# Phases of three pairs, single banks and a two-bank operation for every third maximum, in an attention loop on one core

## The reference

```python
q = proj(Wq, bq)
k = proj(Wk, bk)
v = proj(Wv, bv)
attn = jnp.einsum('bhnd,bhmd->bhnm', q, k) * scale
attn = jax.nn.softmax(attn, axis=-1)
out = jnp.einsum('bhnm,bhmd->bhnd', attn, v)
```

## Time and profile before

| | us |
|---|---|
| median of three runs | 254.62 |
| profiled execution, its own time | 254.18 |
| its span, first to last instruction | 252.4 |
| PE busy | 238.2 (94%) |
| DVE busy | 194.9 (77%) |
| ACT busy | 178.6 (71%) |
| maxima on DVE, L1141, 128 of 1.22 | 155.3 |
| exp on ACT, L979, 232 of 0.60 | 126.0 |
| maxima's matmuls, L437, 256 | 92.7 |
| scores' matmuls, L472, 256 | 89.6 |
| values' matmuls, L530, 1024 records | 80.4 |

### The profile page before, as it was taken

The page is one execution under the profiler, slowest core; times in us unless marked ns, Lnnn a source line. Parts: engine busy times, 40 slices in busy tenths (PEclk is TensorE's granted clock), DMA queues, the critical chain, the costliest instruction groups (busy, mean ns, idle before and its releaser), DMA issues.

```text
span 252.4 us, 5599 instructions
## 1 busy us (share of the span) xinstructions
PE 238.2 (94%) x2105; PEld 109.6 (43%) x2106; DVE 194.9 (77%) x288; ACT 178.6 (71%) x366; POOL 46.4 (18%) x84
## 2 busy tenths in 40 slices
PE   8999998999999999999999999999989988789994
PEld 7455343333334333334343343333333875458420
DVE  2799788989889898898988989889502683359763
ACT  2736697888888888888888888888898132229610
POOL 7964099010010100101001210010100000000340
PEclk9999999999999999999999999999999999999999
DMA  4025300342112031440200000000000000000002
GB/s 135 0 79 170 94 0 4 84 171 68 40 47 68 23 85 39 100 168 5 95 1 3 1 3 2 4 0 4 1 4 1 3 0 3 0 3 0 1 0 86
DMA packets 6099, 10.06 MB, mean 40 GB/s; under 512 B 2240, under 2 KB 3840, under 8 KB 5944
## 3 DMA queue, kind: packets, MB, share of 16 engines
q1 hardware_dynamic: 6072, 9.70, 13.1%
HBM read 6.84 MB, written 2.62 MB: 37 GB/s over the span
## 4 chain that ended last, share of the span: by engine, by line
PE 79%; DVE 7%; POOL 5%; issue 4%; ACT 3%; DVEq 0%; POOLq 0%; ACTq 0%
PE psum L530 25%; PE psum L437 17%; PE psum L472 15%; PE psum L782 2%; PE psum L503 2%; DVE negmax L1141 2%; POOL qop L832 1%; POOL kop L832 1%; PE psum L382 1%; PE psum L540 1%; PE psum L402 1%; PE psum L691 1%; PE psum L496 1%; POOL early L912 1%; PE psum L414 1%
## 5 line engine op out<-in xcount | busy, mean ns | idle before, releaser
L1141 DVE TENSOR_REDUCE negmax<-psum 128x1 f32<-128x1024 f32 x128 | 155.3, 1224 | 14.9 <-PE psum L437 10.5
L979 ACT ACTIVATE probs<-psum 128x512 f32<-128x512 f32 x232 | 126.0, 598 | 19.9 <-PE psum L472 15.8
L437 PE MATMUL psum<-kop,qop 64*128 64x512 f32 x256 | 92.7, 444 | 0.6 <-DVE negmax L1141 0.3
L472 PE MATMUL psum<-qop,kop 64*128 64x512 f32 x256 | 89.6, 445 | 0.1
L530 PE MATMUL psum<-probs,v_aug 128*32 128x256 f32 x1024 | 80.4, 390 | 1.1
L472 PEld LDWEIGHTS psum<-qop,kop 64*128 64x128 f32 x256 | 37.1, 184 | 26.8 <-ACT probs L979 17.8
L437 PEld LDWEIGHTS psum<-kop,qop 64*128 64x128 f32 x256 | 37.6, 184 | 24.5 <-DVE negmax L1141 13.0
L530 PEld LDWEIGHTS psum<-probs,v_aug 128*32 128x32 f32 x1024 | 21.2, 108 | 42.2 <-ACT probs L979 27.2
L867 POOL TENSOR_TENSOR attn<-o_tok,rden 128x64 f32<-128x64 f32 x15 | 4.4, 297 | 105.5 <-DVE rden L1132 105.5
L931 POOL TENSOR_TENSOR early<-probs,early 128x512 f32<-128x512 f32 x4 | 5.1, 1274 | 50.2 <-ACT probs L1077 50.1
L540 PE MATMUL psum<-cbf_sb 128*128 128x256 bf16 x118 | 14.0, 273 | 0.0
(11 more groups left out here) (185 smaller groups left out, 183.4 us busy)
## 6 DMA issues: line engine op xcount, KB each, us to landing
parts_scratch<-early SPq DMA_DIRECT2D x4, 512.0 KB, 3.4
qop<-parts_scratch SPq DMA_DIRECT2D x28, 64.0 KB
vt_sb<-in_vt SPq DMA_DIRECT2D x1, 1024.0 KB, 4.9
kop<-parts_scratch SPq DMA_DIRECT2D x14, 64.0 KB
kop<-parts_scratch SPq DMA_DIRECT2D x28, 32.0 KB
x_sb<-in_x SPq DMA_DIRECT2D x2, 256.0 KB, 2.8
q_pair<-in_q_pairs SPq DMA_DIRECT2D x1, 512.0 KB, 3.3
qop<-max_row SPq DMA_DIRECT2D x28, 4.0 KB
```

The costliest lines, as they stand in the source:

```text
L437: last = nc.tensor.matmul(psum[:, 2 * (v % 2) + c, :], qop[at, b * PP + pp, qh * NH + t * P:qh * NH + (t + 1) * P], kop[at, b * PP + pp, c ...
L472: last = nc.tensor.matmul(psum[:, bank, :], kop[at, b * PP + pp, mt * P:(mt + 1) * P], qop[at, b * PP + pp, qh * NH:(qh + 1) * NH], start= ...
L979: last = nc.scalar.activation(probs[:, n % P_RING, h, :], psum[:, bank, :], ACT.Exp, scale=SCALE)
L1141: V.tensor_reduce(negmax[:, i, h * HT + t:h * HT + t + 1], psum[:, bank:bank + 2, :].rearrange("p a n -> p (a n)"), AX_X, ALU.max, negate= ...
```

## The change

Six things change together.

1. PE's order is written in pairs `p`, four per run, and in phases of three pairs (`PHASE`). Behind each phase come the values that are due: up to half unit p - 4 (`VALUES_LAG`), but never past the end of a block before the phase's end that reaches it (`values_goal`). That is one and a half units as a rule. At the end of a block the numbers are uneven, as the listing below shows.
2. `values(u, first, end)` can do half a unit: four matmuls over 128 columns instead of 256.
3. The four maxima banks are single: half m of a maximum goes to bank m modulo 4, and waits until half m - 4 is reduced.
4. DVE reduces the two halves of a maximum by two operations of 512 columns each (L1220 of the changed kernel), except for every third maximum, where one operation reads both banks and gives two columns (L1214). All go to `half_max`; when a block's maxima are there, one small operation takes the minimum of the two negated halves into `negmax` (L1224) and raises `maxima_done`, for which POOL waits instead of `slot_free`.
5. `CATCH_UP` is (0, 1), so the maxima run two units further ahead, and seven runs at the end have no maxima instead of six.
6. The transposes of maxima and of the output stand at the end of a phase, in front of its values. Before, those of the output also stood in front of values, behind two pairs, and those of the maxima behind values.

The core of the diff:

```diff
-CATCH_UP = (0,)
+PAIRS_OF = 2 * TOGETHER
+PHASE = 3
+VALUES_LAG = 4
+MAX_BANKS = 4
+ROWS_AHEAD = 3
+CATCH_UP = (0, 1)
...
+        for p in range(PAIRS_OF * RUNS):
+            wide = p >= WIDE_PAIR
+            if p % PAIRS_OF == PAIRS_OF - 1 if wide else ends_phase(p):
+                block_end = 2 * TT * (goal // (2 * TT) + 1)
+                goal = max(0, min(block_end, 2 * TOGETHER * (p // PAIRS_OF) if wide else p - VALUES_LAG))
+                values_goal[p] = goal
+                if goal == block_end:
+                    block_done[goal // (2 * TT) - 1] = p
+
+        def rows_pair(blk):
+
+            p = PAIRS_OF * (RUNS_OF * blk - ROWS_AHEAD) + PAIRS_OF - 1
+            return p if p >= WIDE_PAIR else phase_end_from(p)
...
+        def output_pair(blk):
+
+            p = block_done[blk]
+            return p + 2 * (PAIRS_OF if p >= WIDE_PAIR else PHASE)
...
+                m = HALVES * v + c
+                if m >= MAX_BANKS:
+                    pe.wait_ge(S["slot_free"], m - MAX_BANKS + 1)
                 if c == 0:
-                    if v >= 2:
-                        pe.wait_ge(S["slot_free"], v - 1)
...
-                last = nc.tensor.matmul(psum[:, 2 * (v % 2) + c, :],
+                last = nc.tensor.matmul(psum[:, m % MAX_BANKS, :],
...
-                if c == HALVES - 1:
-                    last.then_inc(S["slot_full"], 1)
+                last.then_inc(S["slot_full"], 1)
...
+            def values_until(n):
+
+                while half_units[0] < n:
+                    u, first = divmod(half_units[0], 2)
+                    end = 2 if first or half_units[0] + 2 <= n else 1
+                    values(u, first, end)
+                    half_units[0] += end - first
...
+            def after_pair(p):
+
+                small_work(p)
+                if p in values_goal:
+                    values_until(values_goal[p])
...
-                pool.wait_ge(S["slot_free"], TT * (blk + 1))
+                pool.wait_ge(S["maxima_done"], blk + 1)
...
-                dve.wait_ge(S["slot_full"], v + 1)
-                V.tensor_reduce(negmax[:, i, h * HT + t:h * HT + t + 1],
-                                psum[:, bank:bank + 2, :].rearrange("p a n -> p (a n)"), AX_X, ALU.max,
-                                negate=True).then_inc(S["slot_free"], 1)
+                at = h * HT + t
+                if v % PHASE == 0:
+                    dve.wait_ge(S["slot_full"], HALVES * (v + 1))
+                    first = HALVES * v % MAX_BANKS
+                    V.tensor_reduce(half_max[:, i, :, at], psum[:, first:first + HALVES, :], AX_X, ALU.max,
+                                    negate=True).then_inc(S["slot_free"], HALVES)
+                else:
+                    for c in range(HALVES):
+                        m = HALVES * v + c
+                        dve.wait_ge(S["slot_full"], m + 1)
+                        V.tensor_reduce(half_max[:, i, c, at:at + 1], psum[:, m % MAX_BANKS, :], AX_X, ALU.max,
+                                        negate=True).then_inc(S["slot_free"], 1)
+                if v % TT == TT - 1:
+                    dve.wait_ge(S["slot_free"], HALVES * (v + 1))
+                    V.tensor_tensor(negmax[:, i, :], half_max[:, i, 0, :], half_max[:, i, 1, :], ALU.min).then_inc(S["maxima_done"], 1)
```

More of the change, by code:

```diff
@@ L230, in scores_of, with ends_phase, phase_end_from @@
             return [(a, 0), (b, 0), (a, 1), (b, 1)] if max_jobs(g) else [(a, 0), (a, 1), (b, 0), (b, 1)]
[L232 to L240, removed]
+        def ends_phase(p):
+            return p % PHASE == PHASE - 1
+        def phase_end_from(p):
+            return p + (PHASE - 1 - p) % PHASE
@@ new lines, in conv_attn_hybrid_kernel @@
+        FIRST_WIDE = min(g for g in range(RUNS) if not max_jobs(g))
+        WIDE_PAIR = PAIRS_OF * FIRST_WIDE
+        values_goal, block_done = {}, {}
+        goal = 0
+        for p in range(PAIRS_OF * RUNS):
[6 more added lines that the diff above has]
+                    block_done[goal // (2 * TT) - 1] = p
@@ L242, in conv_attn_hybrid_kernel @@
         ST_JOBS = [("max_r", 0, 0)]
         for g in range(RUNS):
[L244 to L253, removed]
+            for i in range(PAIRS_OF):
+                p = PAIRS_OF * g + i
+                if g < FIRST_WIDE:
+                    ST_JOBS.append(("scores", *scores_of(g)[i]))
+                    ST_JOBS += small_jobs(p)
+                elif i % 2:
+                    ST_JOBS.append(("unit", p // 2, 0))
+                    if i == 1 and rows_within(g) is not None:
+                        ST_JOBS.append(("max_t", rows_within(g), 0))
@@ L254, in conv_attn_hybrid_kernel @@
+            if g >= FIRST_WIDE:
+                for p in range(PAIRS_OF * g, PAIRS_OF * (g + 1)):
+                    ST_JOBS += small_jobs(p)
             if g == 0:
                 ST_JOBS += [("qk", hf, 0) for hf in range(HALVES)]
[L256 to L259, removed]
         st_index = {job: q for q, job in enumerate(ST_JOBS)}
@@ L275, in st_before @@
             return max((p for p in range(q) if set(st_banks(p)) & set(st_banks(q))), default=-1)
+        copies_behind = {}
+        for blk in range(LAST):
+            g, i = divmod(block_done[blk], PAIRS_OF)
+            job = ("scores", *scores_of(g)[i]) if g < FIRST_WIDE else ("unit", TOGETHER * g + 1, 0)
+            copies_behind[st_index[job]] = blk
         def exp_of(u, h):
@@ L467, in scores @@
                     if bank < 4:
-                        pe.wait_ge(S["slot_free"], UNITS - (1 - bank // 2))
+                        pe.wait_ge(S["slot_free"], HALVES * UNITS - (2 - bank))
                 else:
@@ L517, in attn_to_channels, with values @@
                 last.then_inc(S["attn_t_full"], 1)
-            def values(u):
+            def values(u, first, end):
                 blk, mt = divmod(u, TT)
                 b, pp, qh = BLOCKS[blk]
+                n = (end - first) * P
+                at = first * P
                 pe.wait_ge(S["st_done"], max(exp_of(u, h) for h in range(2)) + 1)
@@ L608, in _ @@
                         scores(u, h)
[L609 to L610 removed]
+                    if rows_within(g) is not None:
+                        maxima_to_rows(rows_within(g))
                     for u, h in s[TOGETHER:]:
                         scores(u, h)
[L613 to L620 removed]
+                    for i in range(PAIRS_OF):
+                        after_pair(p + i)
             attn_to_channels(0)
[L623 to L624 removed]
+            values_until(2 * UNITS)
             project(0)
@@ L1001, in _ @@
                 last.then_inc(S["st_done"], 1)
-                if n % TOGETHER == 1 and (kind == "unit" or (kind == "scores" and h == 1)):
-                    g = n // TOGETHER
-                    if g >= RUNS_OF and g % RUNS_OF == 0:
-                        copy_output(g // RUNS_OF - 1)
+                if q in copies_behind:
+                    copy_output(copies_behind[q])
             copy_output(LAST)
```

58 lines of the change are left out of this document (35 added, 23 removed).

## The result

The changed kernel takes 265.35 us, median of four runs (263.24 to 269.94), and the kernel before, run beside it, 254.61 (253.97 to 254.94). The ratio is 1.040, with a 95% interval of 1.032 to 1.048. The change makes the kernel slower, as forecast, but by 10.7 us and not by 4.0; the time lies above the range's 262.5. The profiled execution took 266.32, with a span of 264.5 and a mean clock of 0.981; the two faster ones had 0.987 and 0.993.

A forecast was written before the change was run, and what follows sets the result against it. PE sets the pace before; the change moves the floor to DVE, 9.74 plus 1.0 idle, block 10.75 us. Opening +0.20, blocks +2.1 and tail +1.66 make +3.96: median 258.6, range 252.0 to 262.5.

The forecast's parts named there:

- Prices: Attention loop's assumed costs: third pair 0.23 behind the second, half unit 0.215, phase 1.68, singles 0.60 us.
- the transposes' bank wait: At a phase's end, output transposes wait 0.28 us for the first pair's bank; those of maxima 0.12.
- The half unit's 0.215: PE's values over 128 columns: a half unit costs 0.215 us, bounds 0.215 to 0.43.
- DVE's priced sum: DVE's work per block: eight units 9.40, minimum 0.20, reciprocal 0.12; stated sum 9.74 us.
- The handoff: DVE-PE loop between doubles fills 3.48 of 3.53 us; PE's extra work leaves DVE idle 1.0 per block.
- the 0.19 that spare was to absorb: PE's spare of 0.17 us per two phases takes some 0.19 of 1.20 us of extra waits per block.
- none hidden: Upper bound for a block, with none of the extra waits hidden: 10.94 us.
- Opening: Up to the first transposes of maxima, through POOL: the minimum adds 0.20 us; more unpaired maxima lie under PE's wait.
- Tail: After the last maximum: seven runs without maxima instead of six, adding 1.66 us.
- The handoff hides: Rival in the DVE-PE loop: waits overlap, DVE idles 0.5 per block, block 10.24, total 252.0 us; chance 0.21.
- Half units as dear as whole ones: Rival on PE's values: phase 1.89, PE's block 10.66, total 263.0 us; chance 0.07.
- singles that don't overlap: Rival on DVE: each single costs its whole 0.68 us, block 11.0, total 261.7; chance 0.03.

The follow-up runs named there:

- e3: Changed kernel with the transposes of maxima and output behind their phase's values instead of in front: 259.55 us, ratio 1.020.
- e4: Changed kernel with every half maximum reduced alone, no doubles, and the transposes behind their phase's values: 252.36 us, ratio 0.990 to the kernel before.
- e1: Changed kernel with slot_free counting DVE's operations instead of halves, so a double's wait sits on the reduction itself: 265.72 us.
- e5: Changed kernel with small idle matmuls added where PE waits, 28 in run 1 and 16 before the last split: 263.09 us, ratio 1.033.
- e8: Changed kernel with phases of two pairs and one unit and every maximum a double: 261.07 us, ratio 1.026.
- e7: Changed kernel with maxima 12 steps in front instead of 14: 298.24 us, one run.

## Why the prediction was right in sign and wrong in size

- **Prices: right.** A phase in which PE waits for nothing 1.68, third pair 0.23, singles 0.68 long and 0.60 apart, the transposes' bank wait 0.28 (e3 gives 0.36 back for both kinds, against 0.28 and 0.12 in the sum). The half unit's 0.215 is tested only as a part of the 1.68. DVE's priced sum (9.40, 0.20 and 0.12 are 9.72; the text has 9.74) is borne out by e4: with 16 singles it would be some 9.9, and the block is 10.07.
- **The handoff: the step that failed.** The text built the loop from a double to the next of 1.22, 0.04 to be noticed, "a whole phase of PE, 1.68", 0.50 and 0.04, and found 3.48 of 3.53 filled, with 0.05 to spare. Three of these terms are larger. A double starts 0.11 to 0.14 behind the end of its matmul, because its wait is an instruction of its own. PE's notice of a freed bank is 0.05: the first single behind 96.60 ends at 97.28 (0.68 long), and the weight load that waits for it starts at 97.33:

```profile
97.33 0.18 PEld L485 LDWEIGHTS psum<-kop,qop 64*128 64x128 f32 x1 [0.30 <-DVE half_max L1220]
```

  And the phase in the loop is longer than 1.68, because its third pair needs the bank of the first single behind the double. In the loop from the double at 116.04:

```profile
117.18 2.48 DVE L1220 TENSOR_REDUCE half_max<-psum 128x1 f32<-128x512 f32 x4
117.92 0.18 PEld L485 LDWEIGHTS psum<-kop,qop 64*128 64x128 f32 x1
118.35 0.86 PE L580 MATMUL psum<-probs,v_aug 128*32 128x128 f32 x16
```

  The first single ends at 117.86 and the third pair's load starts at 117.92, together with its matmul and not ahead of it. The values follow 0.43 behind (0.32 in the phase of 1.68), and the phase takes 1.82, from 117.32 to 119.14. The loop is 1.23 + 0.05 + 1.82 + 0.50 + 0.13 = 3.73, and the next double does start at 119.77. DVE's own work in it, a reciprocal included, is 3.65. So plain loops have nothing to spare but lose 0.08 to 0.12 each (95.45, 116.04, 128.51), and the 0.19 that spare was to absorb comes back. The block is 11.02, 0.27 above the forecast and 0.08 above the bound called "none hidden", and by 12 to 13 blocks this is 3.4 us of the 6.8 that are missing. Of the 0.27 a run shows 0.11 (e1, which takes the late start alone away; its phases of this kind still take 1.80 to 1.89). That the longer phase is the other 0.16 is argued from the rows; no run takes it apart.

The 0.04 came from the wrong row. The earlier trace rows start at 27.77, where a maximum does start 0.04 behind its matmul; but the idle times of the regular blocks, as in the earlier trace rows at 85.67, stand behind this matmul of the kernel before:

```profile
85.14 0.39 PE L437 MATMUL psum<-kop,qop 64*128 64x512 f32 x1
```

It ends at 85.53, so the maximum at 85.67 is 0.14 behind. That one, the first of a block, waits for the splitting of older maxima too, and its wait on PE is an instruction of its own; the changed kernel has this at every double. The Trainium skill (Perfetto Trace Analysis, Identifying Dependency Chains) says that an instruction which waits on several engines may have semaphore instructions put in front of it. The kernel before agrees, with 14 of them, one for each block from the third on, as the first row shows. In the changed kernel a double waits on PE alone (seven of eight start no block), and all 43 have one, as the second row shows; in e1 raising by 1 instead of 2 left 5, those of doubles that start a block.

```profile
L1140 DVEq EVENT_SEMAPHORE  x14: 21/21/21, 31.1 to 170.3; - x14
L1212 DVEq EVENT_SEMAPHORE  x43: 21/21/50, 11.0 to 185.8; - x43
```

- **Opening: the sum right, the clock missed.** e5's first transposes start at 43.8 against 43.7; +0.20 was forecast. With the clock as granted, it is 46.0. "That PE has more unpaired maxima in front lies under this wait" was true of their time and not of what PE's waiting among them does to the clock.
- **Tail: 1.66 was too little.** From the last transposes to the end e5 takes 2.7 more than before. The seventh run is 1.66 of it; one more block's output falls into the tail, with transposes of 0.37, and PE waits for `o_sb` twice, 0.47 and 0.51, instead of once for 0.68, which is 0.30. Together 2.3; the other 0.4 stays open. With the clock it was 4.1.
- The ledger in us, for the profiled executions: 5.7 blocks, 0.1 opening, 2.7 tail and 3.6 clock are 12.1, the difference of the spans (264.5 and 252.4). The forecast had 2.1, 0.2, 1.66 and none.
- **Rivals.** "The handoff hides" was given 0.21; e4 shows what it needed: singles and covered transposes, with under 0.2 per block beyond DVE's sum. Half units as dear as whole ones and singles that don't overlap, whose times (263.0 and 261.7) lie nearest to the result, are both refuted by their prices; the time came out high for another reason. The rule of 120 cycles plus columns in the Trainium skill (VectorE: DVE Perf Modes, the TRN2 errata section) disagrees with these runs: queued singles start 0.60 apart, not 0.658. The range ended too low because its upper end was made of block costs alone, with no term for the clock and none for a tail in which another block ends. The sign was forecast by the right mechanism; the term that decides the size, the spare of the loop, was not there.

## What to carry to other kernels

When a loop is filled to within a few hundredths of a microsecond, take each handoff from the row that is of the same kind (first operation of a group or a later one, its wait on itself or in front), and follow every release that lies inside the loop, not only the one that closes it, since 0.1 us decides whether the spare absorbs the extra waits or adds to them. An operation that needs two buffers filled on either side of other work holds its loop open for the length of that work: put both halves together or reduce them alone, and put small work that needs a freed bank behind work that doesn't. Moving work to the front or the tail of a loop is not free because it lies under a wait: ask what the engine does meanwhile, and what clock it is granted afterwards.

## What the runs showed of the hardware that was not expected

- A reduction that waits by an instruction of its own started 0.11 to 0.14 us behind the matmul's end, one that carries its wait 0.03 to 0.07 (e1).
- PE's clock fell to 1.2 GHz behind waits that are short by themselves: one of 0.63 and smaller ones among matmuls in run 1, or one of 1.44 (PE busy 2.22 of 3.70 us). It does not fall each time: behind e1's 1.43 it stayed, and in e8 PE was busy 3.99 of 4.70 us from 29.0 to 33.7 and the clock stayed too. Why one wait brings it down and another doesn't is not shown. In the changed kernel PE was busy 3.87 of 4.70 us ahead of the first stretch; in the kernel before it was 4.65, and the clock stayed. With 44 small matmuls in e5 it was at 2.4 GHz throughout. The Trainium skill (TensorE: Matmul & The Clock Gate, A second HAM failure mode: psum-queue depth-cycling) tells of a kernel whose small idle times between groups of matmuls made the clock fall again and again; e7, with 11 slow stretches and a mean of 0.91, shows a clock that falls again and again too, but behind waits of 2.0 us in the mean and 3.9 at most, which are not small.
- Two edits that both shorten one loop gave more together (0.96 per block) than their sum (0.78). The likely reason is that each was partly hidden behind what the other removes; no run takes this apart.
